# A state-space stage on one core: TensorE's share of each step split into two pieces in two banks, side products spread one to a step

## The reference, cut to what matters

```python
xc = silu(conv(x_z) + conv_b)
dt = clip(softplus(xc @ dt_W + dt_b), 0.001, 0.1)
Bp, Cp = xc @ B_W, xc @ C_W
def step(h, ins):
    dA = exp(dt_t[..., None] * A)
    h = dA * h + dt_t[..., None] * B_t[:, None, :] * x_t[..., None]
    y_t = einsum('ben,bn->be', h, C_t)
y = y * silu(z);  x = x + y @ out_proj_W
```

## Time and profile before

| | |
|---|---|
| median of 3 runs | 6208.38 us (6199.04 to 6209.72) |
| the profiled execution, its own time | 6207.22 us |
| its span | 6205.6 us |
| busy: PE, DVE, ACT, POOL | 82%, 78%, 54%, 54% |
| state-space stage | about 60 to 2315 us of the span |
| exponentials, D products (1008 each), sums A | 1123.0, 892.7, 881.9 us busy |

### The profile page before, as it was taken

The page is one execution under the profiler, slowest core; times in us unless marked ns, Lnnn a source line. Parts: engine busy times, 40 slices in busy tenths (PEclk is TensorE's granted clock), DMA queues, the critical chain, the costliest instruction groups (busy, mean ns, idle before and its releaser), DMA issues. The chain is left out here.

```text
span 6205.6 us, 171083 instructions
## 1 busy us (share of the span) xinstructions
PE 5067.6 (82%) x62308; PEld 2985.9 (48%) x62308; DVE 4814.9 (78%) x8259; ACT 3337.3 (54%) x4892; POOL 3324.8 (54%) x3129
## 2 busy tenths in 40 slices
PE   6999999999999977886866965999967758887890
PEld 2444444444444334564655633666745536666440
DVE  5999999999999985897966355777759948888344
ACT  4666666666666654555751211444447737777440
POOL 4444445444444314665643564555547747877674
PEclk9999999999999998998978987999989969999995
DMA  1111111111111113221122642000001111111443
GB/s 48 50 45 51 45 49 49 47 48 44 52 44 50 43 43 99 54 60 31 43 75 69 152 114 59 19 16 18 15 24 48 49 30 47 47 46 39 148 151 82
DMA packets 584082, 347.70 MB, mean 56 GB/s; under 512 B 63977, under 2 KB 562476, under 8 KB 583468
## 3 DMA queue, kind: packets, MB, share of 16 engines
q1 hardware_dynamic: 562268, 312.85, 17.9%
q0 software_dynamic: 11648, 21.26, 1.8%
q10 hardware_dynamic: 9552, 5.58, 0.3%
HBM read 180.39 MB, written 66.85 MB: 40 GB/s over the span
## 5 line engine op out<-in xcount | busy, mean ns | idle before, releaser
L1434 ACT ACTIVATE mb_dA<-ps,mb_a_neg 128x1024 f32<-128x1024 f32 x1008 | 1123.0, 1114 | 791.9 <-PE ps L1192 791.0
L1870 DVE TENSOR_TENSOR mb_m<-mb_dA,ps 128x704 f32<-128x704 f32 x1008 | 892.7, 886 | 31.5
L1877 DVE TENSOR_TENSOR ps<-mb_m,ps 128x704 f32<-128x704 f32 x992 | 881.9, 889 | 0.1
L1175 PE MATMUL ps<-mb_m,mb_ident 128*32 128x320 f32 x7936 | 741.3, 446 | 7.3
L1224 PE MATMUL ps<-mb_m,mb_cz 128*32 128x256 f32 x8064 | 622.8, 380 | 31.4 <-issue 14.2
L1864 DVE TENSOR_TENSOR mb_m<-mb_dA,ps 128x320 f32<-128x320 f32 x1008 | 484.8, 481 | 87.0 <-PE ps L1175 67.1
L1207 PE MATMUL ps<-mb_ur,mb_bl 64*128 64x256 bf16 x4032 | 388.1, 271 | 49.5 <-DVE mb_m L1870 42.7
L1192 PE MATMUL ps<-mb_ur,mb_sel 64*128 64x256 bf16 x4032 | 396.2, 275 | 19.4 <-DMA mb_ur<-mb_pc 13.8
L1224 PEld LDWEIGHTS ps<-mb_m,mb_cz 128*32 128x32 f32 x8064 | 255.5, 110 | 324.6 <-issue 55.8
L1730 POOL TENSOR_TENSOR mb_ys<-mb_ys,mb_cbu 128x256 f32<-128x256 f32 x64 | 46.8, 731 | 531.0 <-ACT mb_ys L1531 530.0
L703 POOL TENSOR_TENSOR ea_p<-ea_p,ea_rec 128x2048 f32<-128x2048 f32 x70 | 253.5, 3621 | 104.5 <-DVE ea_rec L868 104.5
(11 more groups left out here) (509 smaller groups left out, 13142.8 us busy)
## 6 DMA issues: line engine op xcount, KB each, us to landing
mb_ur<-mb_pc SPq DMA_DIRECT2D x768, 64.0 KB
mb_bl<-mb_pc SPq DMA_DIRECT2D x576, 64.0 KB
ef_w<-in_ef_w SPq DMA_DIRECT2D x35, 515.5 KB
mx_w<-in_mx_w SPq DMA_DIRECT2D x39, 384.0 KB
moe_made<-mx_y SPq DMA_DIRECT2D x39, 256.0 KB, 2.4
ea_x<-hidden SPq DMA_DIRECT2D x280, 32.0 KB, 2.0
pairs<-ea_y SPq DMA_DIRECT2D x70, 128.0 KB, 1.9
ef_tk<-pairs SPq DMA_DIRECT2D x35, 256.0 KB
```

Of the source, the lines that this page charges most:

```text
L1175: mm = nc.tensor.matmul(out[c:c + 32], weights[:, c:c + 32], moving, start=start, stop=stop, skip_group_check=not grouped)
L1434: nc.scalar.activation(dA[:, t % RING].rearrange("p (g n) -> p g n", g=2), ps[:, DT:DT + 2, :], ACT.Exp, scale=a_neg[:, 0:1]).then_inc(dA_ ...
L1870: nc.vector.tensor_tensor(m[:, t % RING, DVE_PART], dA[:, t % RING, DVE_PART], state(u, t - 1, DVE_PART), ALU.mult).then_inc(md_ready.sem, 1)
L1877: nc.vector.tensor_tensor(h, m[:, t % RING, DVE_PART], h, ALU.add).then_inc(hd_ready.sem, 1)
```

## The change

TensorE's 320 columns become two pieces of 160, one at either end of the 1024, so that one lies in the first bank and one in the second. VectorE's order in a step is now F (160 columns), A, **S** (the other 160 columns), D. A has a third wait, for TensorE's second addition of the same step. TensorE's order is now `contract(t-1)`, first addition, [side product if `tl` is 8 or more], second addition, [side product if `tl` is below 8], `ub`, `dt`. The side products of the first quarter move so that there is one to a step (`gates` at 9 to 12, `project_c` at 13, 14, 15 and the next 0), and `turn_u`/`project_bc` of the second quarter one step later. `weigh_bc` moves from VectorE to ScalarE. On ScalarE the copies `take_u` and `take_turn` go ahead of the step's exponential, `take_y` ahead of `take_c`, `take_gates` to `tl` 10 and 12.

```diff
+    UT = [1, 2, 1, 1]
...
-        PE_PART = slice(704, 1024)
-        DVE_PART = slice(0, 704)
+        P_PART = slice(0, 160)
+        Q_PART = slice(864, 1024)
+        DVE_PART = slice(160, 864)
...
                 def products(dt, ub, v):
-                    if dt:
...
                     if ub:
...
-                                                      start=g == 0 or pl == 0, stop=g == 0, skip_group_check=g == 1)
+                                                      start=pl == 0, stop=False, skip_group_check=True)
+                    if dt:
...
-                def add_decayed(i, u, t):
+                def add_first(i, u, t):
                     pe.wait_ge(mp_ready.sem, mp_ready.at(i, t))
-                    by_quarters(state(u, t, PE_PART), ident, m[:, t % RING, PE_PART], False, True, False).then_inc(hp_ready.sem, 1)
+                    by_quarters(state(u, t, P_PART), ident, m[:, t % RING, P_PART], False, True, False).then_inc(hp_ready.sem, 1)
+
+                def add_second(i, u, t):
+                    pe.wait_ge(mq_ready.sem, mq_ready.at(i, t))
+                    by_quarters(state(u, t, Q_PART), ident, m[:, t % RING, Q_PART], False, True, False).then_inc(hq_ready.sem, 1)
...
-                    pe.wait_ge(mp_ready.sem, mp_ready.at(i, t))
+                    pe.wait_ge(mq_ready.sem, mq_ready.at(i, t))
                     pe.wait_ge(md_ready.sem, md_ready.at(i, t))
...
                     for t in range(T):
-                        if 1 <= t < T - 1:
-                            add_decayed(i, u, t)
                         if t >= 2:
                             contract(i, t - 1)
                         elif t == 0 and trail:
                             contract(i - 1, T - 1)
-                        side(i, u, t // 16, t % 16, lead, trail)
+                        if 1 <= t < T - 1:
+                            add_first(i, u, t)
+                        if t % 16 >= 8:
+                            side(i, u, t // 16, t % 16, lead, trail)
+                        if 1 <= t < T - 1:
+                            add_second(i, u, t)
+                        if t % 16 < 8:
+                            side(i, u, t // 16, t % 16, lead, trail)
...
+                def weigh_bc(i, j):
+                    k = 4 * i + j
+                    act.wait_ge(cb_step.sem, cb_step.at(k))
+                    act.wait_ge(cbu_ready.sem, cbu_ready.at(k - 1))
+                    nc.scalar.activation(cb_prod[:], cb_prod[:], ACT.Identity, accum_out=cb[:, 0:1]).then_inc(cb_ready.sem, 1)
...
                     for t in range(T):
                         j, tl = t // 16, t % 16
+                        if j == 0 and lead >= 2 and tl == 8:
+                            take_turn(i + 2)
+                        ip, jp = (i, j + 2) if j < 2 else (i + 1, j - 2)
+                        if tl == UT[j] and (j < 2 or lead):
+                            take_u(ip, jp)
                         if t + 3 < T:
                             decay(i, t + 3)
...
                 def add_part(i, u, t):
                     dve.wait_ge(ub_done.sem, ub_done.at(i, t + 1))
+                    dve.wait_ge(hq_ready.sem, hq_ready.at(i, t))
                     dve.wait_ge(md_ready.sem, md_ready.at(i, t))
...
-                        decay_pe_part(i, u, t)
+                        decay_first(i, u, t)
                         if t >= 2:
                             add_part(i, u, t - 1)
+                        decay_second(i, u, t)
...
                         decay_part(i, u, t)
-                        if tl == 11:
-                            if j < 2:
-                                weigh_bc(i, j + 2)
-                            elif lead:
-                                weigh_bc(i + 1, j - 2)
```

More of the change, by code:

```diff
@@ L1342, in side @@
                     behind = j > 0 or trail
-                    if tl == 1 and ahead:
+                    if tl == UT[j] and ahead:
                         if j == 0 and lead:
@@ L1355, in side @@
                             turn_u(i + 1, j - 2)
-                    if tl == 2 and ahead:
+                    if tl == UT[j] + 1 and ahead:
                         if j < 2:
@@ L1383, in side @@
                                 turn(i + 2)
-                            elif tl == 10:
+                            elif tl == 9:
                                 pe.wait_ge(xT_ready.sem, xT_ready.at(i + 2))
[L1386 to L1389, removed]
+                            if tl in (9, 10, 11, 12):
+                                gates(i + 2, tl - 9)
+                        if lead and tl >= 13:
+                            if lead >= 2 and tl == 13:
                                 pe.wait_ge(gates_taken.sem, gates_taken.at(i + 2))
[L1391 to L1394, removed]
+                            project_c(i + 1, 1 - u, tl - 13)
                     elif j == 1:
@@ L1570, in first @@
                         round_mid(0, j)
+                        weigh_bc(0, j)
                     decay(0, 1)
@@ L1602, in chunk @@
                                 round_mid(ip, jp)
+                            elif tl == 11:
+                                weigh_bc(ip, jp)
                         if tl == 4 and behind:
@@ L1849, in split_lo, with decay_first @@
                         lo_ready.sem, 1)
-                def weigh_bc(i, j):
-                    k = 4 * i + j
-                    dve.wait_ge(cb_step.sem, cb_step.at(k))
-                    dve.wait_ge(cbu_ready.sem, cbu_ready.at(k - 1))
-                    nc.vector.tensor_reduce(cb[:], cb_prod[:], AX.X, ALU.add).then_inc(cb_ready.sem, 1)
-                def decay_pe_part(i, u, t):
+                def decay_first(i, u, t):
                     dve.wait_ge(dA_ready.sem, dA_ready.at(i, t))
@@ L1899, in first @@
                     split_lo(0)
-                    weigh_bc(0, 0)
                     own_rows(1)
@@ L1903, in first @@
                     split_lo(1)
-                    weigh_bc(0, 1)
                     gate_x(1)
```

34 lines of the change are left out of this document (23 added, 11 removed).

## The result

The changed kernel took 6285.66 us (median of 4 runs, 6271.09 to 6290.44) against 6205.65 us for the kernel before on the same chip (4 runs, 6199.04 to 6209.72): ratio 1.0129, 95% interval 1.0116 to 1.0142. It is slower by 80 us, where +30 was forecast (6237, range 6180 to 6300); the time lies inside the range, near its upper end. The profiled execution took 6282.10 us. From the first F to the last D the stage lasts 2303.7 us, before 2226.1: 77.6 of the 80 us lie in it.

What follows compares the result with a forecast made beforehand. VectorE and TensorE both looked full; VectorE's chain set the 2.12 us step, waiting for TensorE only at F. Terms -54 - 8 + 8 - 67 + 43 + 21 + 41 + 19 + 27 = +30 us gave 6237, range 6180 to 6300.

Steps and rivals of the forecast that it cites:

- pace of a step: Every full step: with the split on VectorE a step takes 2.066 us instead of 2.12; -54 us in all.
- old waits at F: Kernel before: F waits for TensorE's addition, 67.1 us in 73 waits; these go as they stand, -67 us.
- (a): Quarter starts: contract, waiting for take_y, holds the first addition, so F waits 1.23 us; +43 and +21 us.
- (b): First quarter: gates 2 and project_c 0 hold the second addition, A waits 1.18 us twice a chunk; with smaller waits +41.
- (c): tl 8 to 15 of other quarters: side products ahead of the second addition make two steps 4.25 against 4.13; +19 us.
- (d): Chunk ends: ub waits for D(63) and stands ahead of dt(2), so F(2) waits 1.6 us; +27 us.
- The swap: TensorE's ub put ahead of dt; its cost was named at chunk ends, a 1.6 us wait where 1.09 was idle before.
- Faster: Rival: ScalarE's copies are taken early enough, or TensorE's lateness stays in its slack; -94 us, 6113; chance 0.12.
- one of (a) and (b) hidden: Rival: only one of the long waits, (a) or (b), shows; -34 or -11 us, 6173 to 6196; chance 0.13.
- Third wait of A: Rival: A's three semaphores cost 0.05 us a step on A alone; 6287; within a slower case of chance 0.13.
- TensorE as the bound of every step: Rival: no step is faster than 2.12 since TensorE sets it; +54 on the sum, 6291; chance 0.04.
- The signs: Trace marks of a right forecast: F to F of 2.07, TensorE-ended idle about 60 us before A, about 85 before F.

Runs made afterwards that it cites:

- e6: Changed kernel plus three unneeded 256-column products filling TensorE's idle time ahead of the contract that waits for take_y at steps 33 and 49; ratio 1.0094 to the kernel before.
- e9: Changed kernel with only the order of ub and dt undone, so dt stands ahead of ub again on TensorE; ratio 0.9984 to the kernel before.
- e4: Changed kernel with A's own wait for ub dropped, leaving A two waits instead of three; ratio 1.0104 to the kernel before.

## Why the prediction was right in sign and 50 us short

Its terms against the changed kernel's trace (waits as medians over chunks 3 to 13, times the chunks that have them):

| term | predicted | measured |
|---|---|---|
| pace of a step | -54 | -65 |
| `weigh_bc` off VectorE | -8 | -8 |
| `output` | +8 | +8 |
| old waits at F | -67 | -67 |
| (a) quarter starts | +64 | +72 |
| (b) first quarter | +41 | +41 |
| (c) side products in the others | +19 | +15 |
| (d) chunk ends | +27 | +30 |
| A at step 61 behind `take_dt` | none | +21 |
| clock at 1.2 GHz | none | +14 to 17 |
| starts of chunks, first chunk | none | +4 |
| not assigned to a step | none | about +12 |
| sum | +30 | +78 |

- **Pace.** An unhindered step is 0.798 + 0.231 + 0.798 + 0.231 = 2.058 against 2.125 before: 0.067 saved, 0.055 predicted from rounded rows. 0.231 for 160 columns is the 0.233 of the slope through the earlier trace rows; the 125 ns of the Trainium skill (Perfetto Trace Analysis, Optimizing Scalar/DVE Operations) would by estimate have made it 0.29. These traces differ: 0.231 for 160 columns and 0.798 for 704 leave a fixed part of 0.064.
- **(a), (d).** The chain of 4.10 us measured 4.04, the chunk end's 3.66 measured 3.62 (D(63) at 1535.10, F(2) at 1538.72), the 160-column addition's 0.52 to its reader 0.54. (a) came 8 higher by small waits behind it (0.1 at A in five steps, 0.22 at step 22).
- **(b).** 2.96 a chunk was predicted and 2.96 measured, though with other parts: 1.16 at 12 and at 14, 0.42 at 9 in place of the estimated 0.5, and 0.12 and 0.1 at 10 and 16; that the sums agree so closely is luck.
- **The step that failed** is (c): "24 steps: 1.35 x 14 = 19". It took all side products at `tl` 8 to 15 of the later quarters for products that only take TensorE's time. The fourth quarter's are `project_dt`, and the fifth of them waits for `take_dt` on ScalarE, exactly as the gate products wait in (b). It was to be read in the code, by the same reasoning: A at step 61 waits 1.49, 21 us in all. The loop of two steps itself was right: 2.087 and 2.166 by turns, 4.25 together as forecast, 15 us in the sum. So the step that failed is that (c) priced no wait of a side product for ScalarE.
- **The clock** had no term, and is the second step that failed. The prediction took the "granted clock of 0.99" of the kernel before as it was; in the changed kernel 14 dips stand in place of 2, most of them behind new idle gaps. e6 puts 14 us on it. These two and the 8 us by which (a) came higher are 44 of the 48 us between +30 and +78; the smaller differences in the table all but cancel.
- **The swap** was charged with (d) alone. e9 shows that it carries 90 us: parts of (a), (b) and (d), all of (c), and the clock. Each chain of the prediction contains "ub 0.99" ahead of `dt`, so the price was in the sum; what it did not do is ask for each chain what it would be without that wait. Undone, the change is a gain of 12 us in the stage (10 by the ratio).
- **Rivals.** Faster, and one of (a) and (b) hidden: excluded, as both waits stand in the trace at their forecast size. Third wait of A, 0.05 a step on A alone, 50 us: its size was right (0.055), but only the steps where the addition ends late pay it, 20 us in all (e4); that the measured 6286 meets this rival's 6287 is luck. TensorE as the bound of every step: excluded by the 439 steps in which A follows F after 0.231.
- **The signs.** The prediction named about 60 us of idle before A, and 61.6 came. That is luck too: about 20 of it is the wait at step 61, which the prediction did not have, and the steps of (c) add almost no idle.

Open: the cause of the 12 us not assigned to a step. Where 11 of them lie can be told: A in 225 steps at 0.254 instead of 0.231 makes 5; in the 553 steps in which A is held at all, S follows it after 0.805 instead of 0.798, 4 more; and step 62 of the fourth, eighth and twelfth chunk and step 15 of the chunk behind each are 0.35 longer than in the other chunks, 2 more, which the kernel before does not show. Whence these intervals come was not found; dropping a wait did not change the 0.254. Nor did any run show why only 11 of the changed kernel's nearly 50 waits of about 1.5 us for `take_y` were followed by a dip.

## What to carry to other kernels

When an in-order engine's work is reordered, list for each instruction that now stands ahead of the critical one every wait that it has, in every phase of the loop, and follow that wait to the other engine's queue: here six waits of 1.2 to 1.5 us all ended in a copy behind a 1.1 us exponential, and moving the copies was worth 137 us, more than the change itself could gain. A product that waits for an instruction's end (`ub`) belongs behind one that does not (`dt`). A finer split on the bound engine pays only when the waits of the engine that feeds it stay hidden at the faster pace: the same split was worth 8 us with the copies behind the exponential and 42 with them ahead of it.

## What the runs showed of the chip that was not expected

- TensorE's granted clock fell to 1.2 GHz for a few microseconds in 14 places, in 11 of them right after it had waited about 1.5 us for `take_y`, in a stage where it is otherwise busy nine tenths; with 0.4 us shorter waits (e9: 1.13 us before `contract`) or filled ones (e6) 2 and 5 were left. Each of the 11 made the steps around it 1.4 to 1.6 us longer in all than the same steps of other chunks, and filling nine of the waits gave back 14 us of the stage (e6).
- An instruction on VectorE that waits for three semaphores starts 0.055 later than one that waits for two when the last one comes late (e4: 0.123 against 0.068 behind the addition's end; F to A 0.33 against 0.27), and no later when all have come (0.231 either way).
- A 704-column product on VectorE lets the next instruction without a wait start 0.798 after its own start, 0.08 before its end; for 160 columns it is 0.231 of 0.315.
